# First attention layer: the softmax division moved out of each group of two heads and done once per half turn, by GpSimd

## What is computed

```python
# x: (2, 1024, 128), 16 heads of 64
q, k, v = (proj(w) for w in (wq, wk, wv))
scores = jnp.einsum('bhqd,bhkd->bhqk', q, k) * 64 ** -0.5
probs = jax.nn.softmax(jnp.where(causal, scores, -jnp.inf), axis=-1)
out = jnp.einsum('bhqk,bhkd->bhqd', probs, v)      # then @ wo.T, (1024 -> 128)
```

## Time and profile before

| | |
|---|---|
| median of 3 runs | 1376.65 us (1375.78 to 1378.95) |
| the profiled execution | 1379.0 us, its span 1377.2 us |
| busy TensorE, weight load, VectorE, ScalarE, GpSimd | 1177.0, 868.5, 958.5, 886.1, 84.8 us |
| first attention | from 40.8 us to 665.3 us |
| mean granted TensorE clock | 0.953 of 2.4 GHz |

### The profile page before, as it was taken

One profiled execution on the slowest core, in us unless ns is written; L12 is line 12 of the kernel. 1 busy time (PEld: TensorE's weight loads), 2 busy tenths in 40 slices (PEclk: granted clock), 3 DMA queues, 4 the chain that ended last, 5 costly groups with the idle time before them and its releaser, 6 DMA issues.

```text
span 1377.2 us, 29673 instructions
## 1 busy us (share of the span) xinstructions
PE 1177.0 (85%) x10570; PEld 868.5 (63%) x10570; DVE 958.5 (70%) x2833; ACT 886.1 (64%) x2124; POOL 84.8 (6%) x89
## 2 busy tenths in 40 slices
PE   3698999989898998989999995458888888888886
PEld 2476766767676776758866774235655655656664
DVE  4566666657666666756452328759999999999963
ACT  2476676757666666756123340548998998998933
POOL 1600000000000000000110003200000000000033
PEclk9899999999999999999979997759999999999999
DMA  4301112120202112110000000241121122020001
GB/s 119 80 23 47 37 48 53 47 53 17 61 23 62 38 47 53 47 47 1 2 31 12 23 11 1 72 89 15 24 36 22 16 36 28 10 36 1 3 1 31
DMA packets 26607, 48.32 MB, mean 35 GB/s; under 512 B 3770, under 2 KB 13650, under 8 KB 26338
## 3 DMA queue, kind: packets, MB, share of 16 engines
q1 hardware_dynamic: 25666, 44.90, 14.8%
q10 hardware_dynamic: 800, 1.57, 0.4%
HBM read 17.10 MB, written 4.19 MB: 15 GB/s over the span
## 4 chain that ended last, share of the span: by engine, by line
PE 55%; DVE 17%; issue 16%; ACT 8%; DMA 2%; POOL 1%; SPq 1%; ACTq 0%; DVEq 0%; POOLq 0%
PE pO L942 12%; PE pT L1001 11%; PE pS L977 9%; DVE Zb L705 9%; PE pT L914 4%; PE pS L1059 4%; ACT probs L520 4%; PE pT L1071 3%; PE pS L1020 2%; PE pT L918 2%; PE pO L931 2%; PE pS L1156 1%; PE pS L981 1%; PE pS L1136 1%; DMA KS<-split 1%
## 5 line engine op out<-in xcount | busy, mean ns | idle before, releaser
L1001 PE MATMUL pT<-cst,probs 128*128 128x128 f32 x2304 | 368.8, 287 | 55.2 <-ACT probs L520 53.7
L1001 PEld LDWEIGHTS pT<-cst,probs 128*128 128x128 f32 x2304 | 250.1, 143 | 141.5 <-ACT probs L520 96.9
L509 ACT COPY PT<-pT 128x512 f32<-128x512 f32 (+3 forms) x597 | 276.0, 485 | 38.3 <-PE pT L1001 35.0
L520 ACT ACTIVATE probs<-pS,nmax 128x128 f32<-128x128 f32 (+7 forms) x256 | 190.6, 745 | 81.6 <-DVE nmax L715 74.3
L942 PE MATMUL pO<-PT,V 128*64 128x128 f32 (+1 forms) x4608 | 230.5, 277 | 0.0
L715 DVE TENSOR_REDUCE nmax<-pS 128x1 f32<-128x128 f32 (+7 forms) x256 | 192.2, 751 | 45.0 <-PE pS L981 41.1
L520 ACT ACTIVATE probs<-Sm,nmax 128x128 f32<-128x128 f32 (+7 forms) x256 | 199.2, 778 | 30.1 <-DVE nmax L722 23.3
L705 DVE TENSOR_SCALAR Zb<-pS 128x128 bf16<-128x128 f32 (+7 forms) x256 | 192.8, 753 | 22.3 <-PE pS L981 22.1
L977 PE MATMUL pS<-Kh,Qs 128*128 128x512 f32 (+2 forms) x384 | 167.7, 440 | 44.8 <-ACT probs L520 37.8
L722 DVE CUSTOM_DVE_ANT_0 Sm<-pS,Zb 128x128 f32<-128x128 f32 (+7 forms) x256 | 192.7, 753 | 5.6
L942 PEld LDWEIGHTS pO<-PT,V 128*64 128x64 f32 (+1 forms) x4608 | 179.9, 113 | 24.0 <-ACT PT L509 0.9
(11 more groups left out here) (173 smaller groups left out, 1365.7 us busy)
## 6 DMA issues: line engine op xcount, KB each, us to landing
Qs<-Ql SPq DMA_DIRECT2D x32, 256.0 KB, 3.7
Kh<-Kh SPq DMA_DIRECT2D x32, 256.0 KB, 3.5
Kl<-Kl SPq DMA_DIRECT2D x32, 256.0 KB, 4.6
QS<-split SPq DMA_DIRECT2D x72, 64.0 KB
KS<-split SPq DMA_DIRECT2D x72, 64.0 KB
w0s<-in_w SPq DMA_DIRECT2D x8, 192.0 KB, 2.4
split<-parts SPq DMA_DIRECT2D x2, 768.0 KB, 3.5
split<-parts ACTq DMA_DIRECT2D x2, 768.0 KB, 12.7
```

The lines of the kernel that those rows point to most:

```text
L509: nc.scalar.copy(PT[:, g % 2, h, k0 * P:(k0 + nk) * P], pT[r % TBANKS][:, 0:nk * P])\
L520: nc.scalar.activation(probs[:, i % NPROB, 0:n], src[:, 0:n], ACT.Exp, bias=nmax[:, i % 4:i % 4 + 1], scale=sign, accum_out=den[:, g % 4, ...
L1001: m = nc.tensor.transpose(pT[r % TBANKS][:, kt * P:(kt + 1) * P], probs[:, item % NPROB, (k0 + kt) * P:(k0 + kt + 1) * P], ident)
```

## The change

For the first attention only:

- ScalarE puts the row sums in `den0`, 128 x (2 halves) x 2 heads x 8 query tiles, instead of `den`. It waits at the first item of a half until the reciprocals of two halves ago have been taken.
- Reciprocal and spread for each group on VectorE, the transpose of `rdb` on TensorE and the copy `rs` on ScalarE are gone. VectorE copies `pO` to `attnT` unscaled as soon as the values are there.
- Once per half, at the second step of the next half, VectorE takes the reciprocals of all 128 x 16 sums (`invert`).
- SyncE then writes these 2048 factors to DRAM, each a run of 4 bytes there since neighbours in a partition are 128 queries apart (`factors`, laid out as head, query). It waits until they have landed and until GpSimd is done with the half before, and reads each head's row of 1024 factors back into 64 partitions of `rsb0` (2 DMAs of 256 KB). `spread(2c)` stands between `halves(c, 1)` and the load of `w0s` for turn c + 1, and `spread(2c + 1)` behind `halves(c + 1, 0)`.
- GpSimd multiplies the half's 128 x 1024 values by `rsb0` in place, once per half (16 times).
- TensorE's output projection waits for GpSimd's last multiplication.

```diff
+        den0 = sb("den0", [P, 2, HPC, ST])
+        rden0 = sb("rden0", [P, 2, HPC, ST])
+        rsb0 = wq_t[:, :, :].rearrange("p t f -> p (t f)")
+        factors = nc.dram_tensor("factors", (CH0 * B, HPC, S), F32, kind="Internal").ap()
...
+            def spread(half):
+                sp.wait_ge(dens_inverted, half + 1)
+                sp.dma_start(factors[half, :, :].rearrange("h (t q) -> q h t", q=P), rden0[:, half % 2, :, :],
+                             allow_slow_non_contiguous=True)\
+                    .then_inc(factors_out, 16)
+                if half == 0:
+                    sp.wait_ge(q_p, 5 * (FC1 + 1))
+                else:
+                    sp.wait_ge(rescaled, half)
+                sp.wait_ge(factors_out, 16 * (half + 1))
+                for h in range(HPC):
+                    sp.dma_start(rsb0[h * DH0:(h + 1) * DH0, :], factors[half, h:h + 1, :].to_broadcast([DH0, S]))\
+                        .then_inc(factors_in, 16)
...
             for c in range(CH0):
                 halves(c, 1)
+                spread(2 * c)
                 if c + 1 < CH0:
                     sp.wait_ge(A[0]["t"], plan.projection(c, 1, 2, 1) + 1)
                     sp.dma_start(w0s[:, :, :], w0[c + 1, :, :, :]).then_inc(ld_w0, 16)
                     halves(c + 1, 0)
+                spread(2 * c + 1)
...
+            for half in range(CH0 * B):
+                values = attnT[:, half % B, half // B, :]
+                pool.wait_ge(A[0]["n"], (half + 1) * ST)
+                pool.wait_ge(factors_in, 16 * HPC * (half + 1))
+                pool.tensor_tensor(values, values, rsb0, ALU.mult).then_inc(rescaled, 1)
...
-                    if plan.ends_group(i - QUEUED):
+                    if k == 1 and plan.ends_group(i - QUEUED):
                         factors_out(a, plan.group(i - QUEUED))
...
+                        if k == 0:
+                            total = den0[:, half % 2, h, qt:qt + 1]
+                            if half >= 2 and at_half == 0:
+                                act.wait_ge(dens_inverted, half - 1)
...
+                    if k == 0:
+                        dve.wait_ge(a["o"], g + 1)
+                        nc.vector.tensor_copy(put(*plan.order[g]), pO[:, 0:P]).then_inc(a["n"], 1)
...
+                def invert(half):
+                    dve.wait_ge(a["p"], (half + 1) * (plan.per // B))
+                    if half >= 2:
+                        dve.wait_ge(factors_out, 16 * (half - 1))
+                    nc.vector.reciprocal(rden0[:, half % 2, :, :], den0[:, half % 2, :, :]).then_inc(dens_inverted, 1)
...
-                    summed = plan.ends_group(i - 2)
+                    summed = k == 1 and plan.ends_group(i - 2)
...
+                    if k == 0 and i >= 2 and (i - 1) % (plan.per // B) == 0:
+                        invert(i // (plan.per // B) - 1)
...
-                pe.wait_ge(a["rd"], g + 1)
-                nc.tensor.transpose(pO[:, P:2 * P], rdb[:, g % 2, :], ident)
+                if k == 1:
+                    pe.wait_ge(a["rd"], g + 1)
+                    nc.tensor.transpose(pO[:, P:2 * P], rdb[:, g % 2, :], ident)
...
-            pe.wait_ge(A[0]["n"], len(L[0].order))
+            pe.wait_ge(rescaled, CH0 * B)
```

More of the change, by code:

```diff
@@ L292, in build @@
         y_done = [sem(f"y_done{k}") for k in range(5)]
+        dens_inverted, factors_out, factors_in, rescaled = (sem(n) for n in ("dens_inverted", "factors_out", "factors_in", "rescaled"))
         names = ["s", "mx", "z", "p", "t", "cp_act", "cp_dve", "rd1", "rd", "o", "rs", "n"]
@@ L515, in attention @@
                             act.wait_ge(a["t"], plan.round_of[i - NPROB] + 1)
-                        if g >= 4 and h == 0:
-                            act.wait_ge(a["rd1"], g - 3)
+                        half, at_half = divmod(i, plan.per // B)
+                        if k == 0:
+                            total = den0[:, half % 2, h, qt:qt + 1]
+                            if half >= 2 and at_half == 0:
+                                act.wait_ge(dens_inverted, half - 1)
+                        else:
+                            total = den[:, g % 4, h:h + 1]
+                            if g >= 4 and h == 0:
+                                act.wait_ge(a["rd1"], g - 3)
                         act.wait_ge(a["mx"], i + 1)
@@ L521, in attention @@
                                              bias=nmax[:, i % 4:i % 4 + 1], scale=sign,
-                                             accum_out=den[:, g % 4, h:h + 1]).then_inc(a["p"], 1)
+                                             accum_out=total).then_inc(a["p"], 1)
             copies_T(0)
@@ L680, in outputs @@
                 def outputs(g):
-                    dve.wait_ge(a["rs"], g + 1)
-                    nc.vector.tensor_tensor(put(*plan.order[g]), pO[:, 0:P], rs[:, g % 2, :], ALU.mult).then_inc(a["n"], 1)
+                    if k == 0:
+                        dve.wait_ge(a["o"], g + 1)
+                        nc.vector.tensor_copy(put(*plan.order[g]), pO[:, 0:P]).then_inc(a["n"], 1)
+                    else:
+                        dve.wait_ge(a["rs"], g + 1)
+                        nc.vector.tensor_tensor(put(*plan.order[g]), pO[:, 0:P], rs[:, g % 2, :], ALU.mult).then_inc(a["n"], 1)
+                def invert(half):
[3 more added lines that the diff above has]
+                    nc.vector.reciprocal(rden0[:, half % 2, :, :], den0[:, half % 2, :, :]).then_inc(dens_inverted, 1)
                 def reciprocals(g):
```

## The result

Four runs of the changed kernel gave 1452.69 to 1462.43 us, median 1457.51; the kernel before gave 1377.80 beside them (median of four). The ratio is 1.0573 [1.0548, 1.0599]: slower by 79.7 us, 70 us beyond the forecast of 1387 and above the end of the range, 1440. The profiled execution took 1462.43 us with a span of 1460.6, 83.4 more than the span before.

A forecast was written before the change was run, and what follows sets the result against it. PE was taken to bound the first attention; a gain of 22 us, stalls of 20.3 us for `w0s` and 11.8 us at the end summed to +10 us, so 1387 us, range 1360 to 1440.

The forecast's parts named there:

- What bounds the kernel: First attention: PE bounds it, busy 576 of 621 us, so work leaving PE is gained, work leaving DVE and ACT hardly.
- The gain of 22 us: First attention: removing 128 transposes of `rdb` gives 20.5 us, shorter waits 1.5; 22 us in all, of 14 to 32.
- The 1.5 us for the relief of ACT and DVE: First attention: less waiting of ACT for reciprocals and a shorter way from values to `n`, 1.5 us, of 0 to 5.
- the two starts that the forecast allowed for the values: PE, per group: without the transpose the values start 0.07 or 0.17 us behind L981 in place of 0.28.
- The order of SP's queue: `w0s` load stands behind `spread(2c)`, so PE stalls W - 2.6 us in each of 7 turns, 20 us in all.
- W: SP's write of 2048 factors to DRAM: time from issue to landing, taken as 5.5 us, bounds 2.3 and 17.7.
- The clock: Output projection's start: after PE's idle time, half clock for 5.3 us costs 2.7 us; per turn counted only at slow writes.
- The end: Before the output projection: PE starts 3.65 + W later, 9.1 us, plus 2.7 us at half clock; 11.8 us.
- The sum: Whole kernel: -22 + 20.3 + 11.8 = +10 us, in general 8W - 34 for W over 2.6; 1387 us.
- the rival with the slow write and clock losses: First attention's turns: from W = 8 each stall also costs 2.7 us of clock; 1442 us at W = 10; chance 0.25.
- The range: Whole time: 1360 us, at W of 2.3 with more gain, up to 1440 us, at W = 10 with clock losses.
- The rival with a cheap write: SP's write: W near 2.3 us, no stalls, -13 us, 1363 us; chance 0.33, shared with more relief.

## Why the prediction was wrong

**What bounds the kernel: right.** What leaves PE is gained, what leaves ACT and DVE is not. The kernel with the transposes kept shows both, at 0.9997 of the time before.

**The gain of 22 us: right in size, in part by luck.** It is 23.1 us by the start of the projection, and 25.8 us by the ratio 0.9813, inside 14 to 32. The 0.16 us for each transpose were taken from the chain. They measured 0.19, of which some 0.05 is clock that the kernel before lost and that the sum had no term for; the transposes' own 0.14 us make some 18 in place of 20.5. The 1.5 us for the relief of ACT and DVE did not come. Of the two starts that the forecast allowed for the values, 0.07 and 0.17 us behind L981, the later one came true (0.16).

**The order of SP's queue: right.** `w0s` was named as what is late next, in 7 turns, with a stall of W - 2.6. At 12.07, the mean W of the seven writes ahead of `w0s`, that is 9.5 us, and 64.4 / 7 = 9.2 were measured; at W = 4.5 it is 1.9, and 1.7 to 2.2 were measured. That `w0s` would share the engines with the reads did not help.

**W: wrong, and this is the step that failed.** The forecast took 5.5 us, from 27 ns for a packet of X, raised to 32. W was 11.7 to 12.5. It lay within the bounds of 2.3 and 17.7, yet the argument for the value was at fault twice. It took the price to be one per packet on a busy engine, and the engines had finished 3 us after the issue, with 9 us still to go. And it took as nearest a row of large packets that land each in its own place, while what counts is where the small ones land: spread out, these 2048 runs take 3.9 to 4.5 us and the forecast's way of counting would nearly have held. No row of the kernel before has small writes side by side. The Trainium skill's fixed 2.0 us plus bytes over 436 GB/s ("Anatomy of one DMA", GpSimd's path) gives 2.0 for this write, and on SP's queue it fits neither: 12 us as it is, and 1.46 in runs of 64 bytes. With nothing to show the price, 5.5 of 2.3 to 17.7 was too near the low end for the main case.

**The clock: priced rightly, put in the wrong case.** 2.7 us were counted for the end, where 31.78 less 28.85 is 2.9. The same 2.7 us in each turn stood in the rival only. It was paid: the low clock cost some 19.6 us in the kernel after, about 12 more than before, and about 18 more than with nothing divided.

**The end: right in form.** 3.65 + W is 15.6 for W = 11.97; it grew from 3.7 to 19.7 us, by 16.0. POOL took 2.34 us for 2.55.

**The sum.** What happened is the rival with the slow write and clock losses, at a chance of 0.25. Its formula at W = 12 is -22 + 7 x (9.4 + 2.7) + 3.65 + 12 + 2.7 = +81 us, and +79.7 was measured. From the kernel with nothing divided to the kernel after, by the start of the projection, it is 64.4 (stalls) + 16.8 (the end, 19.7 for 2.9) + 18.3 (clock) = 99.5, where 742.38 less 642.55 is 99.8. In the profiled execution the later start, 76.7 us, and the projection's own 2.9 us more make 79.7 as well. So the one term that was mis-sized explains the miss: 8 us for each us of W, on 6.5 us, is 52, and the clock in 7 turns is 19, together 71 of the 70 us missed.

**The range: too narrow.** Its upper end stood at W = 10, with bounds worked out to 17.7. Each us of W moves the time by 8, and nothing in the profile spoke against 12.

The rival with a cheap write did not come true, though its arithmetic did: at W = 1.46 its formula, -22 + 3.65 + 1.46 + 2.7, gives -14 us, and the runs of 64 bytes were at 0.9888, which is -15.4.

## What to carry to other kernels

- A DMA that waits for another one's landing holds up all that stands behind it in its issuing queue. Ask of each entry behind it when it is needed. Here moving one load ahead of the wait was worth 85 us, and the change's arithmetic was sound otherwise.
- The write of single elements to DRAM could here be priced neither by bytes nor by packets on the engines. Where elements lie side by side, each written by another run, expect the landing long behind the engines' last work, as here by 9 us, and keep both it and its reader off the path; or give every partition a contiguous run, 12 to 1.5 us here. Where such a write has no row in the profile, let the range go to the bound.
- Work that is put off to the end of a stage comes back in full at its last step. Do the last piece in the old way.

## What the runs showed of the hardware that was not expected

- 2048 runs of 4 bytes to DRAM take 10.6 to 12.5 us side by side, 14.2 at 8 bytes from one to the next, 10.4 at 16, 5.5 at 32, 4.4 at 64 and 3.9 to 4.3 from 128 to 512 (from 8 up with the rows of 128 runs 64 KB apart); 3.0 into SBUF; 128 runs of 64 bytes take 1.5. While the slow ones land, the engines' share is 0.01 for 9 us.
- The landing of 512 such runs took 8.4 to 9.7 us, little less than that of four times as many.
- A stall of 9 us took the granted clock to 1.2 GHz, with PE back at full speed some 5 us after its restart. So did an idle time of 6.8 us ahead of the output projection, which then took 30.7 us in place of 28.85; of six stalls of 1.7 to 2.2 us five did not, and one, of 2.09 us, did.
- The kernel before loses some 7 to 8 us by five dips of the clock, 3 to 4 us each, with no wait of PE over 1.2 us ahead of them. The page's mean clock of a stage (0.98) is the only trace of them there, and experiments that take out PE's work or its waits can take such dips out as well.
